# One attention and expert layer on one core: feed-forward pieces in other pairs behind all four value projections, weight splits spread out, bias rows made on all partitions

## The reference

```python
x = x + attn(layernorm(x))      # x is (16, 512, 256)
#   q, k, v = xn @ Wq.T, xn @ Wk.T, xn @ Wv.T        16 heads of 64
#   sim = 50 * tanh((q @ k.T) / 8 / 50); causal; softmax; @ v; @ Wo.T
x = x + ffn(layernorm(x))
#   shared = gelu(t @ sw1 + sb1) @ sw2 + sb2
#   probs = softmax(t @ gate_w + gate_b); the two largest of 8 per token
#   h = gelu(t @ w1[e] + b1[e]); y = h @ w2[e] + b2[e]
#   routed = sum over the two chosen experts of prob * y
#   result = routed + shared
```

## Time and profile before

| | |
|---|---|
| median of 3 runs | 2083.72 us (2082.68 to 2085.25) |
| the profiled execution's own time | 2080.42 us |
| its span | 2078.6 us |
| PE busy | 1922.9 us (93%) |
| DVE, ACT, POOL busy | 1527.5, 1415.6, 1030.0 us |

### The profile page before, as it was taken

How to read it: one execution, slowest core, us unless ns; L and a number is a source line. 1 busy time by engine, 2 the same in 40 slices (tenths; PEclk the granted TensorE clock), 3 DMA queues, 4 the chain that set the end, 5 groups by cost and what they waited for, 6 DMA issues and landing times.

```text
span 2078.6 us, 39943 instructions
## 1 busy us (share of the span) xinstructions
PE 1922.9 (93%) x14653; PEld 1517.5 (73%) x14653; DVE 1527.5 (73%) x2803; ACT 1415.6 (68%) x2170; POOL 1030.0 (50%) x1195
## 2 busy tenths in 40 slices
PE   6799999999999999999999999999999873999998
PEld 4576767676767676767676767676767652999998
DVE  5576878787878787878787878787876885565565
ACT  6677777777777777777777777777777731544444
POOL 3344454545454545454545454545454643444444
PEclk9999999999999999999999999999999995999999
DMA  4000010101010101010101010101010124764664
GB/s 132 1 11 11 11 42 11 42 11 42 11 42 11 42 11 42 11 42 12 41 13 40 14 39 15 38 16 37 16 37 6 37 72 134 232 189 132 196 183 140
DMA packets 73665, 112.51 MB, mean 54 GB/s; under 512 B 9715, under 2 KB 52218, under 8 KB 73476
## 3 DMA queue, kind: packets, MB, share of 16 engines
q1 hardware_dynamic: 58468, 67.86, 11.3%
q0 software_dynamic: 15008, 42.10, 5.4%
HBM read 63.10 MB, written 48.65 MB: 54 GB/s over the span
## 4 chain that ended last, share of the span: by engine, by line
PE 81%; ACT 12%; DVE 5%; issue 2%; DMA 1%; POOL 0%; SPq 0%; POOLq 0%; DVEq 0%
PE bank_o L1239 12%; PE ring L1218 7%; PE ring L1145 6%; PE ring L1151 6%; PE ring L1146 6%; PE ring L1197 6%; PE ring L1223 6%; ACT prob L585 3%; PE acc L1262 3%; PE ring L1204 3%; PE acc L1264 3%; PE acc L1270 3%; ACT prob L591 2%; PE bank_d L1253 2%; PE ring L1404 2%; PE ring L1409 2%
## 5 line engine op out<-in xcount | busy, mean ns | idle before, releaser
L508 POOL TENSOR_SCALAR_AFFINE_SELECT prob<-prob 128x256 f32<-128x256 f32 x512 | 231.1, 473 | 567.7 <-ACT prob L591 567.6
L585 ACT ACTIVATE prob<-ring 128x1024 f32<-128x1024 f32 (+1 forms) x384 | 326.3, 875 | 205.5 <-PE ring L1223 202.3
L591 ACT ACTIVATE prob<-prob 128x1024 f32<-128x1024 f32 (+1 forms) x384 | 342.7, 915 | 5.2
L520 POOL TENSOR_TENSOR key_sum<-prob 128x768 f32<-128x768 f32 x128 | 243.0, 1898 | 205.6 <-PE bank_d L1253 193.9
L1239 PE MATMUL bank_o<-prob,v 128*32 128x512 f32 (+3 forms) x4096 | 306.6, 440 | 25.1 <-DVE weighed L801 14.4
L1218 PE MATMUL ring<-qT,kT 128*128 128x256 f32 (+3 forms) x1024 | 240.2, 336 | 64.7 <-ACT qT L608 20.0
L780 DVE TENSOR_TENSOR kT<-ring,kT 64x512 fp32r<-64x512 f32 x256 | 176.3, 689 | 153.6 <-ACT kT L598 146.8
L1218 PEld LDWEIGHTS ring<-qT,kT 128*128 128x128 f32 x1024 | 166.6, 191 | 146.5 <-issue 71.2
L1239 PEld LDWEIGHTS bank_o<-prob,v 128*32 128x32 f32 x4096 | 118.0, 110 | 185.1 <-issue 159.1
L796 DVE RECIPROCAL norm<-bank_d 128x512 f32<-128x512 f32 x64 | 214.9, 3357 | 21.7 <-PE bank_d L1253 20.1
L1223 PE MATMUL ring<-q_lo,kT 128*128 128x256 f32 (+3 forms) x1024 | 229.6, 326 | 0.9 <-DVE q_lo L785 0.9
(11 more groups left out here) (224 smaller groups left out, 4689.7 us busy)
## 6 DMA issues: line engine op xcount, KB each, us to landing
xin<-first SPq DMA_DIRECT2D x71, 257.0 KB, 3.1
xin<-second SPq DMA_DIRECT2D x71, 129.0 KB, 2.3
xin<-base SPq DMA_DIRECT2D x71, 128.0 KB, 2.5
x_next<-in_x SPq DMA_DIRECT2D x16, 512.0 KB, 4.6
x_res<-in_x SPq DMA_DIRECT2D x16, 512.0 KB, 4.0
raw_e<-in_w SPq DMA_DIRECT2D x4, 1024.0 KB, 6.7
first<-pad SPq DMA_DIRECT2D x9, 257.0 KB, 4.4
second<-pad SPq DMA_DIRECT2D x9, 129.0 KB, 7.5
```

The lines of the kernel that those rows point to most:

```text
L508: last = nc.gpsimd.affine_select(out=diag, in_=diag, compare_op=ALU.is_ge, fill=0.0, base=0, pattern=[[0, 2], [1, P]], channel_multiplier=-1)
L520: nc.gpsimd.tensor_tensor(sums[:, :, :], t0[:, :, P:N], t13[:, :, 0:N - P], ALU.add).then_inc(sum_steps, 1)
L585: nc.scalar.activation(probs[p % PROBS][u][:, :, :], slot[:, :, 0:UNIT_COLS[u]], ACT.Tanh, scale=SCALE / SOFTCLAMP).then_inc(act_emptied, 1)
L591: nc.scalar.activation(cols, cols, ACT.Exp, scale=SOFTCLAMP).then_inc(exp_done, 1)
```

## The change

- The feed-forward pieces of the sequence before stand in other pairs: `turn2` in pair 2 (was 4), `gate` and `turn_logits` in pair 3 (was 5), `hidden` in pair 4 (was 5), `count_earlier` in pair 5 (was 7). `shared_out` stays in pair 7.
- All four value projections stand in pair 1, with output projections 6 and 7 of the sequence before between them. Output projection 0 moves ahead of the q and k projections in pair 4.
- VectorE's and ScalarE's matching steps move with them. The second layer norm stands whole in pair 1; of the first, the statistics stand in pair 1 and the Newton steps and the normalisation in pair 2.
- GpSimd sends the first rows behind pair 0 (was 1), and the second rows in pair 7 of the next sequence (was pair 2 of the one after).
- In the first sequence only the first 128 columns of w_k and w_q get their low parts before pair 0, the rest behind `empty_qk(0, 0)`. The other weights are split by both engines in the same pairs: w_v in 0, w_o in 2, w_1 in 3, w_2 in 4. The next sequence's layer norm moves from pair 1 to pair 3.
- The biases b1, b2 and sb2 are loaded as 34 columns on 128 partitions, split by two instructions of VectorE, and laid out as rows by six transfers on SP's queue, ahead of the first load of the next x. `prepare_bias` and its four loads go.

The core of the diff:

```diff
-V_UNITS = {1: (0, 1, 2), 2: (3,)}
-FFN_UNITS = {4: ("turn2",), 5: ("gate", "hidden"), 7: ("out",)}
-LATE_UNITS = {5: "logits", 7: "pos"}
+V_UNITS = {1: (0, 1, 2, 3)}
+FFN_UNITS = {2: ("turn2",), 3: ("gate",), 4: ("hidden",), 7: ("out",)}
+LATE_UNITS = {3: "logits", 5: "pos"}
...
-BIAS_STEPS = 5
+LATER_SPLIT = {0: 2, 2: 3, 3: 4, 4: 5}
...
-        sp.dma_start(sb2_part[0][:, :], sb2_twice).then_inc(small_loaded, 16)
+        sp.dma_start(bias_raw[:, :], bias_cols).then_inc(small_loaded, 16)
+sp.wait_ge(bias_split, 2)
+sp.wait_ge(const2_ready, 1)
+for m, part in enumerate(bias_part):
+    for k in range(K):
+        sp.dma_start(b_rows[k * QD + m:k * QD + m + 1, :].bitcast(F32),
+                     part[:, k * BIAS:(k + 1) * BIAS].bitcast(F32)).then_inc(bias_placed, 16)
+    sp.dma_start(sb2_rows[m:m + 1, :].bitcast(F32),
+                 part[:, 2 * BIAS:].bitcast(F32)).then_inc(bias_placed, 16)
-    else:
-        sp.wait_ge(ring_full, AT["turn1", i, 0, 0] + 1)
-        sp.dma_start(b_raw[0], b1_twice[:, 0:E * D // 2]).then_inc(bias_loaded, 16)
-for n, (src, half) in enumerate([(b1_twice, 1), (b2_twice, 0), (b2_twice, 1)]):
-    sp.wait_ge(bias_steps, BIAS_STEPS + 4 * (n + 1))
-    at = half * E * D // 2
-    sp.dma_start(b_raw[(n + 1) // 2], src[:, at:at + E * D // 2]).then_inc(bias_loaded, 16)
...
-        if p == 1 and i >= 2:
+        if p == 0 and i >= 2:
-        if p == 2 and i >= 2:
-            send_second(i - 2)
+        if p == 7 and i >= 1:
+            send_second(i - 1)
-send_second(NSEQ - 2)
...
-split_hi(2)
-        if i == 0 and p == PROBS - 1:
-            act.wait_ge(bias_steps, BIAS_STEPS - 1)
-        if i >= 1 and p == 6:
+        if i >= 1 and p == 4:
...
-if p == 4 and i >= 1:
+if p == 2 and i >= 1:
     copy_x2_hi(i - 1)
...
-if i == 0 and p <= 2:
-    split_hi(3 + p)
+if i == 0 and p in LATER_SPLIT:
+    split_hi(LATER_SPLIT[p])
-if i >= 1 and p == 5:
+if i >= 1 and p == 4:
...
+def split_lo_part(k, part):
+    name, _ = parts[k]
+    dve.wait_ge(hi_split, k + 1)
+    hi, lo, src = (w[:, :].rearrange("p (c f) -> p c f", c=DC)[:, :, part]
+                   for w in (split[name][0], split[name][1], raw[name]))
+    return nc.vector.tensor_tensor(lo, src, hi.bitcast(F32), ALU.subtract)
...
-split_lo(0)
+for k in range(2):
+    split_lo_part(k, slice(0, P)).then_inc(lo_first, 1)
-split_lo(1)
-split_lo(2)
+for k in range(2):
+    split_lo_part(k, slice(P, HD)).then_inc(lo_split, 1)
+nc.vector.tensor_copy(bias_part[0][:, :], bias_raw[:, :]).then_inc(bias_split, 1)
+dve.wait_ge(bias_split, 1)
+nc.vector.tensor_tensor(bias_part[1][:, :], bias_raw[:, :], bias_part[0][:, :].bitcast(F32),
+                        ALU.subtract).then_inc(bias_split, 1)
-def prepare_bias(n):
...
+nc.vector.tensor_copy(earlier[:, :], earlier_f).then_inc(ones_copied, 1)
+def begin_next(i):
+    dve.wait_ge(xnext_loaded, 16 * (i + 1))
+    layernorm_stats(1, x_next)
+    layernorm_guess(1, i)
+def end_next(i):
+    layernorm_newton(1, i)
+    layernorm_apply(1, i, x_next, x_next, xn_ready)
...
     chunk = None
-if i >= 2 and p == 0:
-    empty_pos(i - 2)
-if i >= 1 and p == 6:
+if p == 2 and 1 <= i < NSEQ - 1:
+    end_next(i + 1)
+if p == 4 and i >= 1:
     empty_logits(i - 1)
+if p == 6 and i >= 1:
+    empty_pos(i - 1)
 if i == 0 and p == 3:
...
     weigh_values(*chunk)
-if p == 0 and i >= 2:
-    place_tokens(i - 2)
 if p == 1 and i >= 1:
     split_values(*chunk)
-if p == 2 and i >= 1:
-    split_values(i - 1, PAIRS - 1)
-if p == 3 and i >= 1:
-    layernorm_guess(2, i - 1)
-    layernorm_newton(2, i - 1)
+if p == 4 and i >= 1:
+    choose(i - 1)
+if p == 5 and i >= 1:
+    split_hidden(i - 1)
 if p == 6 and i >= 1:
-    split_hidden(i - 1)
-    choose(i - 1)
+    place_tokens(i - 1)
 if p + 1 < PAIRS:
...
     empty_qk(i + 1, 0)
-if p == 4 and i >= 1:
+if p == 2 and i >= 1:
     empty_turned2(i - 1)
-if p == 5 and i >= 1:
+if p == 3 and i >= 1:
     empty_gate(i - 1)
...
             split_values(*chunk)
-        if i == 0 and p <= 1:
-            split_lo(3 + p)
-            if p == 1:
-                split_lo(5)
+        if i == 0 and p in LATER_SPLIT:
+            split_lo(LATER_SPLIT[p])
+        if i == 0 and p == 3:
+            begin_next(1)
+            end_next(1)
         if p == 1 and i >= 1:
             weigh_values(i - 1, PAIRS - 1)
-        if p == 2 and i >= 1:
+            if i + 1 < NSEQ:
+                begin_next(i + 1)
+            split_values(i - 1, PAIRS - 1)
             add_attention(i - 1)
-        if p == 1 and i + 1 < NSEQ:
-            dve.wait_ge(xnext_loaded, 16 * (i + 2))
-            layernorm_stats(1, x_next)
-            layernorm_guess(1, i + 1)
-            layernorm_newton(1, i + 1)
-            layernorm_apply(1, i + 1, x_next, x_next, xn_ready)
-        if p == 3 and i >= 1:
+            layernorm_guess(2, i - 1)
+            layernorm_newton(2, i - 1)
             normalise_rows(i - 1)
-        if i == NSEQ - 1 and p in (4, 5, 6, 7):
-            prepare_bias(p - 4)
-empty_pos(NSEQ - 2)
-place_tokens(NSEQ - 2)
 last_i = NSEQ - 1
...
 pe.wait_ge(xn_hi, 1)
-project_qk(0, 0, (lo_split, 1), (lo_split, 2))
-MIDDLE = {4: turn2, 5: gate, 7: shared_out}
-LATE = {5: (hidden, turn_logits), 7: (count_earlier,)}
+project_qk(0, 0, (lo_first, 1), (lo_first, 2))
+MIDDLE = {2: turn2, 3: gate, 4: hidden, 7: shared_out}
+LATE = {3: turn_logits, 5: count_earlier}
 for i in range(NSEQ):
...
             scores(i, p, u)
-        if p > 4:
+        if p >= 4:
             project_out(i, p - 4)
-        elif i >= 1 and p < 3:
+        elif i >= 1 and p < 2:
             project_out(i - 1, p + 4)
-        if p + 1 < PAIRS:
+        if i == 0 and p == 0:
+            project_qk(0, 1, (lo_split, 1), (lo_split, 2))
+        elif p + 1 < PAIRS:
             project_qk(i, p + 1)
...
             project_qk(i + 1, 0)
-        if p == 4:
-            project_out(i, 0)
         if i >= 1 and p in MIDDLE:
...
-for t in V_UNITS.get(p, ()):
-    project_v(i, t)
-if p == 2 and i >= 1:
-    project_out(i - 1, PAIRS - 1)
+    project_v(i, 0)
+    if i >= 1:
+        project_out(i - 1, PAIRS - 2)
+    project_v(i, 1)
+    if i >= 1:
+        project_out(i - 1, PAIRS - 1)
+    project_v(i, 2)
+    project_v(i, 3)
...
-if i == 0 and p == 2:
+if i == 0 and p == 3:
-    pe.wait_ge(bias_steps, BIAS_STEPS)
+    pe.wait_ge(ones_copied, 1)
+    pe.wait_ge(bias_placed, 16 * 6)
-    for piece in LATE[p]:
-        piece(i - 1)
+    LATE[p](i - 1)
...
-"sb2_twice": twice(L0_ffn_sb2),
-"b1_twice": twice(L0_ffn_b1),
-"b2_twice": twice(L0_ffn_b2),
+"bias_cols": laid(np.concatenate([np.asarray(b).reshape(P, -1) for b in (L0_ffn_b1, L0_ffn_b2, L0_ffn_sb2)], 1)),
```

More of the change, by code:

```diff
@@ L119, in block_program @@
 def block_program(nc, x, wqT, wkT, wvT, woT, gate_w, gate_b_rows, w1s, w1, w2s, w2,
-                  b1s_cols, sb2_twice, b1_twice, b2_twice, out):
+                  b1s_cols, bias_cols, out):
     first = nc.dram_tensor("first", (ROWS, FIRST_ROW), F32).ap()
@@ L179, in block_program @@
         b_rows = sb("b_rows", [P, E * D], F32R)
+        BIAS = E * D // P
+        bias_raw = sb("bias_raw", [P, 2 * BIAS + D // P])
+        bias_part = [sb(f"bias_{s}", [P, 2 * BIAS + D // P], F32R) for s in ("h", "l")]
         ln = {}
@@ L230, in block_program @@
             pad = sb("pad", [P, ROW], F32, arena)
-            sb2_part = [sb(f"sb2_{s}", [K, D], F32, arena) for s in ("raw", "part")]
         head_rows = [slice(0, DH), slice(DH, P)]
-        b_raw = [x_next[at:at + K, :, :].rearrange("p t d -> p (t d)") for at in (0, QD)]
         earlier_f = norm[:, 0:P]
@@ L282, in block_program @@
         e_lo = sem("e_lo")
-        bias_loaded = sem("bias_loaded")
+        bias_split = sem("bias_split")
+        bias_placed = sem("bias_placed")
         pad_ready = sem("pad_ready")
```

32 lines of the change are left out of this document (2 added, 30 removed).

## The result

The changed kernel takes 2110.67 us (median of 4 runs, 2105.56 to 2113.23) where the kernel before takes 2083.26 us (4 runs): 1.0133 times as long, 95% interval 1.0118 to 1.0149. It is slower by 1.3%; forecast were 2046 us and faster. The profiled execution took 2111.0 us with a span of 2109.3 us.

The account below looks back on a forecast made before the run. TensorE, busy 1922.9 of 2078.6 us, was taken to bound the kernel, with small waits each step. Terms -9 - 3 - 10.5 - 15.2 = -37.7 us gave 2046 us; 8 in 10 range 2026 to 2062.

Parts of the forecast that it names:

- the term for the steady sequence: Each steady sequence: waits fall from 4.46 to 4.0 us; taken as -0.7 us, 15 times, 10.5 us in all.
- the wait for the counts' slot: Second unit of pair 6's scores: VectorE empties the counts' slot only after splitting chunk 2, a wait of 0.95 us.
- port sharing: VectorE's layer norm normalisations beside GpSimd's key sums, 2.1 us to spare before pair 3's k low part: cost nothing.
- fourth value copy; gelu; values 0: Steady waits: 0.63 us for the value copy stays; gelu's 1.01 and the 0.55 before pair 0's values product go.
- gateT and q_lo at the logits: Pair 3: TensorE waits 0.21 + 1.0 us, as VectorE writes q's low part and then gateT.
- logits' slot, second unit of pair 4: Pair 4's scores: VectorE splits chunk 0 before it empties the logits, a wait of 0.55 us.
- q_lo at S(6): Start of pair 6's scores, whose slot is paired with the q/k slot: a wait of 0.55 us for q's low part.
- First sequence: Weight splits and layer norm spread out: gains of 12.9 us less late pieces, -9 us net, bounds 5 and 13.
- Second sequence: Stall of 1.98 us at the start of pair 4's scores (S(4)) goes with what hangs on it: -3 us.
- Last sequence: Without the bias work, fewer waits for weighed values up to the last transposes: -15.2 us, bounds -9 and -18.
- Slower: Rival: VectorE late to pair 3's k low part, layer norm beside GpSimd's sums; 4.5 us a sequence, 2113 us; chance 0.05.
- Rival 2: New slot waits in steady sequences mostly absent: 1.6 us more gained a sequence, 2022 us; chance 0.12.

Follow-up runs that it names:

- e2: Changed kernel with VectorE emptying the slots of the logits and of the position counts before it splits the weighed chunk: 2039.83 us, 0.9777 of before.
- e14: Changed kernel with the logits' slot alone emptied before the split: 2086.20 us, 1.0005 of before.
- e7: Changed kernel with the position counts' slot alone emptied before the split: 2032.89 us, 0.9763 of before.
- e10: The kernel of e2 (changed kernel, both slots emptied early) run again in another job: 2049.22 us, 0.9838 of before.
- e11: e10 with GpSimd's sends of `second` moved behind pair 1's key sums: 2024.97 us, 0.9708 of before.
- e5: Kernel before with one unused tile of 8 columns (32 bytes a partition) behind b_rows: 2088.33 us, 1.0024 of before.
- e3: Changed kernel with three more matmuls a sequence, results overwritten, in front of TensorE's wait for gateT: 2090.15 us, 1.0026 of before.
- e13: Changed kernel with GpSimd's sends of `second` moved behind pair 1's key sums, nothing else: 2089.34 us, 1.0018 of before.
- e15: The kernel of e7 (changed kernel, counts' slot alone emptied early) run again in another job: 2063.82 us, 0.9894 of before.
- e1: Changed kernel's ends (weight splits in the first sequence, bias rows) with the steady order of the kernel before: 2072.16 us, 0.9932 of before.
- e6: e2 with an unused tile of 8 columns that puts the tiles behind it back on multiples of 64 bytes: 2012.99 us, 0.9659 of before.
- e16: Changed kernel with both slots emptied early, tiles on multiples of 64 bytes, sends of `second` behind pair 1's key sums: 2015.71 us, 0.9662 of before.

## Why the prediction was wrong

The failed step is the term for the steady sequence: -0.7 us, 15 times. It came out as +3.6. In a step without a fall (105.42) TensorE waits 105.42 - 100.31 = 5.1 us, against 4.07 before, and works 0.6 longer; the rest, 2.0 on average, is falls of the clock but for 0.1. So three terms failed: the wait for the counts' slot was sized at half, since port sharing had been put at nothing; the wait beside GpSimd's sends was put at nothing; and a wait was priced at its own length, without the clock. Of the 4.3 us a sequence between forecast and result the waits have 1.1, longer work 0.6 and the falls 2.0. The remaining 0.6 lie in the reckoning: it has 4.46 us of waits before, where TensorE stands 4.07 (103.80 - 99.73; the 0.4 for the counts at pair 0 is no wait in the trace), and it took -0.7 between a sum of -0.5 and one of -0.85.

| piece of the steady term | forecast, us | measured, us | shown by |
|---|---|---|---|
| fourth value copy; gelu; values 0 | 0.63; gone; gone | 0.63; gone; gone | waits |
| gateT and q_lo at the logits | 1.2 | 0.82 | waits |
| logits' slot, second unit of pair 4 | 0.55 | 0.65 | e2, e14 |
| q_lo at S(6) | 0.55 | 0 | waits |
| counts' slot, second unit of pair 6 | 0.95 | 1.79 | e2, e7 |
| tanh beside the sends, pair 0 | 0 | 0.85 to 1.5 | e10, e11 |
| placement of tiles | 0 | 0.4 | e5 |
| fall of the clock | 0 | 2.0 on average | e2, e3, e13 to e15 |

- **The slot waits.** Their places were right but for q_lo at S(6). That the sum over gateT, logits, q_lo and counts came out (3.26 forecast, 3.26 measured) is luck: the four miss by -0.38, +0.10, -0.55 and +0.84. At pair 6 the size was off, because I had the split at its undisturbed length: I cost port sharing at nothing after going over the layer norms alone. Those did stay unstretched (all 128 normalisations of L770 take 405 to 417 ns), but the split is longer by 0.96 us, about half of that wait.
- **What I had weighed wrongly** was what a wait costs. I priced 1 us of wait at 1 us. Behind waits that gather at one place TensorE also lost 1.5 us of clock. The waits of before come to 4.07 us in sum and bring none: the longest is 1.10 us, and e1 and e5 with the same waits have no fall either.
- **GpSimd's sends.** The forecast named them only as a bound of the last sequence. Each moved DMA was to be counted where it now stands: here beside the one pair boundary at which ScalarE is awaited.
- **First sequence** -9 forecast, -9.0 measured. The 7.91 us wait is gone, and none above 2.0 us is left between 40 and 90 us. The exact hit is partly luck: with the same start the other profiles have -7.5 to -10.7, and no run takes the pieces apart. **Second sequence** -3 forecast: in e6 it takes 101.19 us and the steady ones 101.15, so the stall at S(4) is gone as reasoned; in the changed kernel the longer step hides it (105.43).
- **Last sequence** -15.2 forecast to the last transposes: 112.34 us in the changed kernel, -7.8; e1 has -11.0, e2 -14.8. The bias work was a cause, since e1 takes away nothing else there: of 14.4 us in four waits for weighed values 5.4 in two are left, and one of 4.7 in the changed kernel (about 3 forecast). It has 11.0 of the 15.2; the whole is reached only about, in e2, which also has the new order without its slot waits. The changed kernel lost the rest as its steady steps lost theirs.
- **Rivals.** Slower had a chance of 0.05 and came true by another mechanism: k's low part was on time in pair 3, and TensorE has no wait for it there. Rival 2 (the slot waits mostly absent) would have given 2022; e16, in which both late slots are emptied early and the sends moved, takes 2016.

Of the whole difference of 30.7 us between the spans, the first two sequences have -10.5, 13 steps +46.6, the last -7.8, and what follows the last transposes +2.3.

## What to carry to other kernels

A wait is not worth its own length only: look whether the granted clock falls behind it, and compare steps that should be alike, since levels a fixed distance apart give the fall away. A slot handed to another engine should be emptied before that engine turns to work that nobody awaits yet; two moved calls won 67 to 71 us here. An instruction's length is to be taken from where it will stand, beside what the other engines do there, and not from its shortest case. When tiles are added, keep the ones behind them where they were.
